# Linear attention with the logarithm and exponential of two chunks taken at once, and dual attention with its norm a group ahead and its result turned in another bank

## The reference

```
scores = jnp.einsum('bqh,bkh->bqk', Q_char, K_sub) * scale
char2sub = jnp.einsum('bqk,bkh->bqh', jax.nn.softmax(scores, axis=-1), V_sub)
scores2 = jnp.einsum('bqh,bkh->bqk', Q_sub, K_char) * scale
sub2char = jnp.einsum('bqk,bkh->bqh', jax.nn.softmax(scores2, axis=-1), V_char)
gate = jax.nn.sigmoid(jnp.einsum('blh,oh->blo', gate_in, Wg) + bg)
return gate * char2sub + (1 - gate) * sub2char
```

```
Qn = _layernorm(Q, ln1_g, ln1_b)          # Kn, Vn likewise from the context
qn = _l2norm(q)                           # q / max(|q|, 1e-12), per head
kn = _l2norm(k)
attn = jnp.einsum('bhqd,bhkd->bhqk', qn, kn)
out = jnp.einsum('bhqk,bhkd->bhqd', attn, v)
x = Q + out @ wo + bo
xn = _layernorm(x, ln2_g, ln2_b)
h = jax.nn.gelu(xn @ w1 + b1, approximate=False)
return x + h @ w2 + b2
```

## Time and profile before

| | |
|---|---|
| median of 3 runs | 4989.81 us (4973.43, 4989.81, 4993.12) |
| the profiled execution | 4968.36 us, its span 4966.6 us |
| TensorE busy | 3972.4 us (80%) |
| VectorE, ScalarE, GpSimd busy | 2442.7, 1741.6, 1295.0 us |
| mean granted TensorE clock | 0.858 of full |
| dual attention | from about 3007 to 3173 us |
| linear attention | from about 3803 to 4452 us |

### The profile page before, as it was taken

One profiled execution on the slowest core, in us unless ns is written; L12 is line 12 of the kernel. 1 busy time (PEld: TensorE's weight loads), 2 busy tenths in 40 slices (PEclk: granted clock), 3 DMA queues, 4 the chain that ended last, 5 costly groups with the idle time before them and its releaser, 6 DMA issues. The chain is left out here.

```text
span 4966.6 us, 79327 instructions
## 1 busy us (share of the span) xinstructions
PE 3972.4 (80%) x32633; PEld 2590.3 (52%) x32633; DVE 2442.7 (49%) x5117; ACT 1741.6 (35%) x2555; POOL 1295.0 (26%) x1130
## 2 busy tenths in 40 slices
PE   5978899989998999855655557427776888889998
PEld 3645677767765566422222224315555666667776
DVE  3645322247656555588888883453333343332222
ACT  3422333311104322333333333211112777754443
POOL 3434100012115200054454443102222232210111
PEclk8978899999999999977777777656666999989999
DMA  3000000000000000000000000000000000000000
GB/s 122 2 1 1 1 1 1 1 30 3 3 29 12 3 1 1 36 0 0 0 0 0 0 0 1 1 0 1 1 1 9 4 6 4 1 1 3 5 5 7
DMA packets 20278, 37.13 MB, mean 7 GB/s; under 512 B 848, under 2 KB 17488, under 8 KB 19280
## 3 DMA queue, kind: packets, MB, share of 16 engines
q1 hardware_dynamic: 19920, 32.07, 1.8%
HBM read 29.97 MB, written 2.10 MB: 6 GB/s over the span
## 5 line engine op out<-in xcount | busy, mean ns | idle before, releaser
L163 PEld LDWEIGHTS ps<-L_ffn_w,arena 128*128 128x128 f32 x5248 | 615.4, 193 | 58.3 <-issue 45.0
L163 PE MATMUL ps<-L_ffn_w,arena 128*128 128x128 f32 x5248 | 627.0, 277 | 0.0
L1958 POOL TENSOR_TENSOR arena<-arena 128x512 f32<-128x512 f32 x256 | 444.2, 1764 | 532.9 <-DVE arena L1919 402.2
L1843 PE MATMUL ps<-arena,const_w 128*128 128x512 f32 x512 | 338.5, 799 | 257.9 <-DVE arena L1927 257.9
L649 POOL TENSOR_SCALAR arena<-arena 128x4 f32<-128x4 f32 x96 | 22.2, 231 | 1847.2 <-DVE arena L641 1846.6
L1935 DVE TENSOR_TENSOR_SCAN arena<-arena 128x512 f32<-128x512 f32 x256 | 483.8, 1931 | 9.3 <-POOL arena L1958 9.3
L751 PE MATMUL ps<-arena,L_ffn_w 128*128 128x512 f32 x1024 | 464.3, 596 | 0.0
L785 DVE SCALAR_TENSOR_TENSOR x_all<-ps,arena,x_all 128x128 f32<-128x128 f32 x512 | 144.2, 345 | 400.8 <-PE ps L163 400.8
L1843 PEld LDWEIGHTS ps<-arena,const_w 128*128 128x128 f32 x512 | 105.8, 227 | 429.2 <-DVE arena L1927 386.2
L751 PEld LDWEIGHTS ps<-arena,L_ffn_w 128*128 128x128 f32 x1024 | 186.2, 192 | 186.4 <-issue 183.9
L163 PEld LDWEIGHTS ps<-L_attn_w,arena 128*128 128x128 f32 x1664 | 231.0, 212 | 94.0 <-issue 43.7
(11 more groups left out here) (352 smaller groups left out, 7209.7 us busy)
## 6 DMA issues: line engine op xcount, KB each, us to landing
L_ffn_w<-L_ffn SPq DMA_DIRECT2D x1, 4312.0 KB, 14.0
L_ffn_w<-L_ffn SPq DMA_DIRECT2D x1, 4120.5 KB, 15.3
arena<-ctx SPq DMA_DIRECT2D x16, 256.0 KB, 3.2
L_ffn_w<-L_ffn SPq DMA_DIRECT2D x1, 3460.0 KB, 11.4
L_attn_w<-L_attn SPq DMA_DIRECT2D x1, 3153.0 KB, 21.0
L_attn_w<-L_xattn SPq DMA_DIRECT2D x1, 2692.0 KB, 9.3
x_all<-x SPq DMA_DIRECT2D x8, 256.0 KB, 4.9
arena<-mask SPq DMA_DIRECT2D x8, 256.0 KB, 3.6
```

Source lines behind the costliest of these rows:

```text
L163: ins = pe.matmul(out, src[:, j * P:(j + 1) * P], w, start=(i == 0), stop=(bias is None and i == len(chunks) - 1))
L1843: pe.matmul(e.bank(6 + c), e.ident, hc(c, n), start=(n == 0), stop=(n == N - 1)).then_inc(s["acc_mm"], 1)
L1958: g.tensor_tensor(bu(c, n), du(c), bs(n), ALU.mult).then_inc(s["bu_done"], 1)
```

## The change

Both steps are edited; nothing in the other ten is.

In linear attention the logarithm and the exponential are done in every odd iteration for two chunks together, on 1024 columns in place of 512. `heads`, `outs` and `output` move one iteration later, so that the factors of a pair are there; the buffers for that grow (`q` and `rn` to four, `ms` to three), and the context input and `x2` shrink to one buffer each. `attended` moves from c = 1 to c = 2, `context_scale` from c = 2 to c = 1, and GpSimd does the norm's factor in front of the residual in c = 2.

```
-                if k >= 1:
-                    heads(k - 1)
+                if k >= 2:
+                    heads(k - 2)
                 if k + 1 < n:
                     query_sums(k + 1)
-                if k >= 2:
-                    output(k - 2)
+                if k >= 3:
+                    output(k - 3)
...
+            heads(n - 2)
+            output(n - 3)
             heads(n - 1)
...
             def factors(k):
-                a.wait_ge(s["b1_cp"], use1["ss", k] + 1)
-                a.activation(rn(k), rn(k), ACT.Ln).then_inc(s["ln_done"], 1)
-                a.wait_ge(s["ln_done"], k + 1)
-                a.activation(rn(k), rn(k), ACT.Exp, scale=-0.5).then_inc(s["rn_done"], 1)
+                a.wait_ge(s["b1_cp"], use1["ss", k + 1] + 1)
+                a.activation(rn2(k), rn2(k), ACT.Ln).then_inc(s["ln_done"], 1)
+                a.wait_ge(s["ln_done"], k // 2 + 1)
+                a.activation(rn2(k), rn2(k), ACT.Exp, scale=-0.5).then_inc(s["rn_done"], 1)
...
-                factors(k)
+                if k % 2 == 1:
+                    factors(k - 1)
...
-                if c == 1 and g >= 1:
+                if c == 2 and g >= 1:
                     l2.rstd(p_, g - 1)
-                if c == 2 and g >= 1:
                     residual(g - 1)
...
-                if k >= 1:
-                    outs(k - 1)
+                if k >= 2:
+                    outs(k - 2)
...
-                if c == 1 and g >= 1:
+                if c == 2 and g >= 1:
                     attended(g - 1)
-                if c == 2 and g + 1 < NG:
+                if c == 1 and g + 1 < NG:
                     context_scale(g + 1)
                     ln.stats(v, g + 1)
```

```
-        xn, xnT = room.take(GT), room.take(GT)
+        xn_b, xnT = room.pair(GT), room.take(GT)
...
             def project(g):
...
+                if g >= 3:
+                    pe.wait_ge(s["x_done"], g - 2)
...
             def turn_z(g):
                 pe.wait_ge(s["z_done"], g + 1)
-                pe.wait_ge(s["b5_cp"], dual_use("z", g))
-                transpose_group(pe, e, e.bank(5), z(g)).then_inc(s["b5_mm"], 1)
+                pe.wait_ge(s["v_cp"], min(g + 3, NG))
+                if g >= NG - 2:
+                    pe.wait_ge(s["x_done"], g)
+                transpose_group(pe, e, e.bank(2), z(g)).then_inc(s["zt_mm"], 1)
...
-            normed(0)
-            normed(1)
+            for g in range(3):
+                normed(g)
             for g in range(NG):
-                normed(g + 2)
+                normed(g + 3)
                 difference(g)
...
-                v.tensor_tensor(e.X(g), e.bank(5), e.X(g), ALU.add).then_inc(s["b5_cp"], 1)
+                v.tensor_tensor(e.X(g), e.bank(2), e.X(g), ALU.add).then_inc(s["x_done"], 1)
```

More of the change, by code:

```diff
@@ L1433, in norm_attention_mlp @@
         room = Room(e.arena)
-        three = lambda t: lambda k: t[:, (k % 3) * GT:(k % 3 + 1) * GT]
-        q, rn, og = three(room.take(3 * GT)), three(room.take(3 * GT)), three(room.take(3 * GT))
-        q2, k2, kn, vs, ms = (room.pair(GT) for _ in range(5))
+        ring = lambda n: (lambda t: lambda k: t[:, (k % n) * GT:(k % n + 1) * GT])(room.take(n * GT))
+        q, og, ms = ring(4), ring(3), ring(3)
+        rn_all = room.take(4 * GT)
+        rn, rn2 = (lambda k: rn_all[:, (k % 4) * GT:(k % 4 + 1) * GT]), (lambda k: rn_all[:, (k % 4) * GT:(k % 4 + 2) * GT])
+        q2, k2, kn, vs = (room.pair(GT) for _ in range(4))
         xn, xnT, n2 = room.pair(GT), room.pair(GT), room.take(GT)
-        c_in, cn = room.pair(GT), room.take(GT)
-        x2, xm, xmT, hid = room.pair(GT), room.take(GT), room.take(GT), room.take(FC * GT)
+        c_in, cn = room.take(GT), room.take(GT)
+        x2, xm, xmT, hid = room.take(GT), room.take(GT), room.take(GT), room.take(FC * GT)
         kss, krn = room.pair(8), room.pair(8)
         ln = TwiceNorm(e, s, room, e.X, xn, 1e-5, lambda g: n2, 1e-5, xnT, e.bank(0), W("ln1_g"), W("ln1_b"))
-        lc = PipedNorm(e, s, room, c_in, lambda g: cn, 1e-5, pre="lc")
-        l2 = PipedNorm(e, s, room, x2, lambda g: xm, 1e-5, pre="l2")
+        lc = PipedNorm(e, s, room, lambda g: c_in, lambda g: cn, 1e-5, pre="lc")
+        l2 = PipedNorm(e, s, room, lambda g: x2, lambda g: xm, 1e-5, pre="l2")
         @block.sync
@@ L1771, in _ @@
                     mlp_out(g - 1)
+            outs(n - 2)
             outs(n - 1)
@@ L1961, in dual_use @@
 def dual_use(step, g):
[L1964 to L1965 removed]
+    return {"p": 2 * g, "gate": 2 * g + 1}[step]
 def dual_attention(nc, e, W):
@@ L1996, in turn @@
                     pe.wait_ge(s["ln_xn"], NT * g + j + 1)
-                    ins = pe.transpose(out[:, j * P:(j + 1) * P], xn[:, j * D:(j + 1) * D], e.ident)
+                    ins = pe.transpose(out[:, j * P:(j + 1) * P], xn_b(g)[:, j * D:(j + 1) * D], e.ident)
                 ins.then_inc(s["pr_mm"], 1)
@@ L2194, in residual @@
             def residual(g):
-                v.wait_ge(s["b5_mm"], dual_use("z", g) + 1)
-                v.tensor_tensor(e.X(g), e.bank(5), e.X(g), ALU.add).then_inc(s["b5_cp"], 1)
+                v.wait_ge(s["zt_mm"], g + 1)
+                v.tensor_tensor(e.X(g), e.bank(2), e.X(g), ALU.add).then_inc(s["x_done"], 1)
             v.tensor_scalar(hb, W("bg"), 0.5, None, ALU.mult).then_inc(s["hb_done"], 1)
-            ln.stats(v, 0)
-            ln.stats(v, 1)
+            for g in range(3):
+                ln.stats(v, g)
             for g in range(NG):
```

46 lines of the change are left out of this document (23 added, 23 removed).

## The result

The changed kernel takes 4916.55 us, median of 4 runs (4915.58 to 4931.79). The kernel before, run beside it, takes 4981.62 (median of 4). The ratio is 0.9878, with a 95% interval of 0.9842 to 0.9915. The forecast was 4926, within 4894 to 4970, and rested on a gain of 64 us; the medians differ by 65.

What follows compares the result with a forecast made beforehand. Serial steps, so the edited stages decide: query sums wait for ScalarE in linear attention, starved transposes and low clock in dual attention. -29 and -35 make -64 us: 4904 from the profiled 4968.4, 4926 as median, range 4894 to 4970.

Steps and rivals of the forecast that it cites:

- the granted clock: Dual attention, sign to look for: granted clock above 0.9, where the profile before had 0.76.
- the bound of -12: Dual attention: if the clock pattern stays, only the waits go, 6 x (1.4 + 0.5), stage -12 us.
- The small price of the residual ahead of the gates: Dual attention: moving the residual from ahead of the gates gives 0.4 us a group at lower clock, nothing at upper.
- c = 5 to 6: even, less 2.58: 6.6: Linear attention, between query sums of a steady group: 9.21 us loses its 2.58 us wait, leaving 6.6.
- My bound of 11 us: Linear attention: if c = 5, 6 and 7 all fall to 1.2 GHz, the stage gains only 11 us.
- c = 7 to 0: Linear attention, between query sums of a steady group: stays at 13.59 us, its slow product kept.
- The upper bound of 41 us: Linear attention: if no product falls to 1.2 GHz, a group gains 6 us and the stage 41.
- 4908: Rival "more than forecast", both stages: no slow product in linear attention, dual clock 1.0, -41 - 38; chance 0.08.
- The order of GpSimd's queue in c = 3 (+1.1): Linear attention, c = 3 to 4: norm's factor and residual ahead of key factors add 1.1 us, giving 7.75.
- Dual clock stays low: Rival, dual attention: clock remains low, so -12 - 29 = -41 us, 4949; chance 0.15.
- The wide pair gives back what it takes: Rival, linear attention: slow c = 5 and 7 and GpSimd's queue leave about 3 us gain, 4952; chance 0.13.
- Slower: Rival, linear attention: long waits pull its clock to 0.76, +36 us, 5026; slower from about 0.83; chance 0.05.

Runs made afterwards that it cites:

- fill_turn: Kernel before plus two identity transposes ahead of each quarter of the normed `x` from group 2 on: dual attention 141.3 us, whole 4960.35 us in one run.
- norms_ahead: Kernel before with dual attention's second buffer and norms three groups ahead, result still turned in bank 5: dual attention 130.3 us (-34.1).
- fill_sums: Changed kernel plus 20 identity transposes ahead of the query sums that wait in c = 5 and c = 7: linear attention 610.8 us, 16.7 less.
- residual_late: Changed kernel with GpSimd's residual in c = 3, behind that iteration's key factors, not in c = 2: linear attention 627.6 us, as without the edit.
- pair_last: Changed kernel with the two-chunk logarithm and exponential issued last in odd iterations, behind turned copies too: linear attention 620.9 us, median 4914.21, ratio 0.9886.
- single_last: Changed dual attention, linear attention of the kernel before with one-chunk logarithm and exponential issued last in each iteration: linear attention 638.3 us, median 4933.33, ratio 0.9922.

## Why the prediction was right, and where it was off

**The total** hit for nearly the right reasons: 4926 forecast, 4916.55 measured. Of the 9 us between them, 8 lie in the starting point: I put the forecast on the shown median of 4989.81, and the kernel before measured 4981.62 beside the changed one. The gain was 64 forecast and 65 between medians, but the trace accounts for 54.9 of it in the edited stages; the 95% interval (0.8 to 1.6%, some 42 to 79 us) holds both, so the agreement to one microsecond is luck.

**Dual attention**: -35 forecast, -34.4 measured, nearly each part as worked out: the start 2.9 us (3), group 6 2.7 (2.6), group 13.29 (13.4), outs 2.00, gates 1.98, no wait of the turn behind group 0. The five groups gained 29.0 in place of 30, since the first gates stayed slow. One sign failed: the granted clock is 0.88 and not above 0.9, as the start, the first gates and the last group are still at the lower level. The choice that carried it, upper clock against the bound of -12, is now shown and not argued: `fill_turn` gives 23 us with the waits' causes in place, and `norms_ahead` all of it. The small price of the residual ahead of the gates is right too: nothing at the upper clock, 3.2 us at the lower (0.4 a group).

**Linear attention**: -29 forecast, -20.4 measured. The mis-sized term is "c = 5 to 6: even, less 2.58: 6.6". It measured 8.2 (9.40 in group 1), since behind the wait of 3.44 us ahead of c = 5 the products run at 1.2 GHz for about 3 us; `fill_sums` brings it to 6.59. I had carried over from the earlier trace rows that the first long waits of a row leave the clock up. That is one group's picture: in group 1 of the same kernel the first wait of 2.58 us, in c = 4, already has sums of 1.62 us behind it. My bound of 11 us, for c = 5, 6 and 7 all slow, took this case in.

From the stage's start to c = 0 of group 1 it gained 7.0 us (4 forecast, for group 0), groups 1 to 6 gained 15.1 (27 forecast), and the last group with the tail lost 1.6 (2). Of the 12 us that groups 1 to 6 lack, c = 5 to 6 has 9 and c = 7 to 0 has 3: that was to stay at 13.59 and rose to 14.9 to 15.0 in groups 3 and 6. The misses of the other intervals cancel. The upper bound of 41 us was a slip besides: its own terms, 6 x 6 + 4 - 2, give 38, which lifts the 4908 and the 4894 by 3 and changes nothing else.

**Other terms.** The order of GpSimd's queue in c = 3 (+1.1) shows in its interval to 0.1 us. But `residual_late` shows that taking it away gains nothing: the transposes of c = 4 then wait as long for VectorE's floors, and I had not looked at what comes behind. The loads and the wide activation were right, and the later heads, outs and output cost nothing that the intervals show.

**Loads and clock.** A load is followed at once by its activation: the pair from 3962.11 to 3966.74 is filled by two loads of 1.28 us and two activations of 1.06. The drain that the Trainium skill, ScalarE: Activation LUTs, What ACT_TABLE_LOAD costs, adds to it is seen in no run here. Of the clock the rows now say that a wait of 3.4 us was followed by products at 1.2 GHz in each of groups 1 to 6. The Trainium skill, TensorE: Matmul & The Clock Gate, HAM oscillation, says the same of waits between bursts. I gave that rule the weight of a bound; for c = 5 it was the answer. The Trainium skill, TensorE: Matmul & The Clock Gate, A second HAM failure mode: psum-queue depth-cycling, describes another kernel, in which frequent short idle times between groups of matmuls have the clock go up and down. That is like dual attention's turn: four waits of 0.16 to 0.45 us in 2.5 us.

**The rivals.** "Dual clock stays low" is out by the outs at 2.00. "The wide pair gives back what it takes" came true in one of its two conditions (c = 5 and 7 slow; GpSimd's queue cost the 1.1 us of the forecast and not 2 more), and was over-priced: it would have left 3 us, and 20 came. "Slower" is out: granted clock 0.93, against 0.94 before and 0.83 where it would have turned. What no rival said is that the edit attacks the smaller half of its own problem: the 20 us of the linear edit stood beside 71 us from the order of the same instructions, which I did not price although shows the waits and my own text named their cause.

## What to carry to other kernels

When a waited-for instruction stands behind long work on its engine, ask first whether the long work can stand elsewhere in that engine's list, and only then whether there can be less of it: here the order was worth 71 us, the edit that takes two chunks at once 20, and both together 74. The place that worked was where the engine had idled, so look for the instruction with a wait in front of it and put the work ahead of it, not behind. And price a wait of TensorE with what runs behind it: the same wait, filled with transposes that nobody reads, cost 23 us less in a stage of 164.

## What the runs showed of the hardware that I had not expected

- Four waits of 0.16 to 0.45 us with single transposes of 0.3 us between them were enough to have the outs behind them at 1.2 GHz (3.20 us against 2.00). With 8 transposes of the identity among them, so that the waits left were 0.15 to 0.23 us, the outs took 2.00. One wait of 0.78 us every 13.3 us left the clock up. A single wait of 1.37 us ahead of the first gates was followed by gates of 3.54 us in the changed kernel and of 1.98 in `fill_turn`.
- Waits of 2.6 us left the clock up twice in a row, waits of 3.4 us in none of groups 1 to 6 of the changed kernel. But the length of the wait alone doesn't decide: in `pair_last` a wait of 2.37 us has sums of 1.90 to 2.00 us behind it in groups 2 to 6, and in `single_last` the first wait of 2.58 us in a row has 1.84 to 2.05 in four groups and 1.10 in two. What decides is not shown by these runs. The fall doesn't always show on the instruction right behind the wait (1.10 us, and then 1.76 for products of 1.05), so the sums' own duration under-counts it.
- A program's unedited stages differed by up to 19 us between profiles, while the two stages studied repeated within 1.3 us (linear attention with its old code within 0.4). An effect of 3 us is read from the stage, not from the whole.
